# ScalarE's high halves of y for the first two groups, eight steps earlier, in a fused attention and feed-forward kernel

## The reference

```
q, k = l2norm(x Wq'), l2norm(x Wk')      # 16 heads of 16 values
attn = softmax(q k' - slope_h * distance), over the 128 keys up to and with the query
x = layernorm(x + (attn v) Wo')
h = gelu(x (alpha1 * sign(w1))' + b1)     # 1024 hidden values, alpha the mean |w| of a row
x = layernorm(x + h (alpha2 * sign(w2))' + b2)
```

## Time and profile before

| | |
|---|---|
| median of 3 runs | 369.43 us (369.34 to 369.77) |
| the profiled execution, its time | 370.22 us |
| its span, first to last instruction | 368.4 us |
| TensorE busy | 353.2 us, 96% of the span |
| VectorE busy | 308.7 us, 84% |
| ScalarE busy | 307.3 us, 83% |
| GpSimd busy | 285.4 us, 77% |
| granted TensorE clock, mean | 0.997 of full |

### The profile page before, as it was taken

How to read it: one execution, slowest core, us unless ns; L and a number is a source line. 1 busy time by engine, 2 the same in 40 slices (tenths; PEclk the granted TensorE clock), 3 DMA queues, 4 the chain that set the end, 5 groups by cost and what they waited for, 6 DMA issues and landing times. The chain is left out here.

```text
span 368.4 us, 13096 instructions
## 1 busy us (share of the span) xinstructions
PE 353.2 (96%) x4461; PEld 244.1 (66%) x4461; DVE 308.7 (84%) x771; ACT 307.3 (83%) x532; POOL 285.4 (77%) x440
## 2 busy tenths in 40 slices
PE   8789999999999999999999999999999999999992
PEld 5555676667766776776677677675666667667682
DVE  5977899898898898898899988879777887786775
ACT  3588888898898998898899999988888888887753
POOL 1188999889989999998999999757756856856433
PEclk9999999999999999999999999999999999999998
DMA  7678944744655646667767773303303513413113
GB/s 231 143 117 186 185 109 98 157 99 94 137 120 106 142 96 132 139 159 154 156 144 155 153 147 74 59 4 59 59 0 59 115 45 72 114 39 76 59 59 114
DMA packets 106884, 40.19 MB, mean 109 GB/s; under 512 B 92128, under 2 KB 105824, under 8 KB 106720
## 3 DMA queue, kind: packets, MB, share of 16 engines
q1 hardware_dynamic: 106848, 39.73, 49.6%
HBM read 12.72 MB, written 4.19 MB: 46 GB/s over the span
## 5 line engine op out<-in xcount | busy, mean ns | idle before, releaser
L1341 POOL TENSOR_SCALAR_AFFINE_SELECT prob<-prob 128x512 f32<-128x512 f32 x252 | 153.7, 646 | 11.1 <-ACT prob L700 11.1
L700 ACT ACTIVATE prob<-ps 128x1024 f32<-128x1024 f32 (+1 forms) x128 | 122.2, 1009 | 13.5 <-PE ps L390 13.4
L551 PE MATMUL ps<-yT,sgn 128*128 128x512 f16 x256 | 61.1, 379 | 0.0
L772 ACT ACTIVATE ps<-ps,bias,alpha 128x512 f32<-128x512 f32 x64 | 47.9, 750 | 15.6 <-PE ps L551 12.5
L421 PE MATMUL ps<-wqkv,xt 128*128 128x512 f32 x124 | 58.7, 596 | 1.2 <-DVE qkn L952 1.1
L411 PE MATMUL ps<-prob,vdiag 128*17 128x128 f32 x1024 | 51.3, 274 | 0.3
L411 PE MATMUL ps<-prob,vnext 128*17 128x128 f32 x992 | 49.9, 273 | 0.0
L1409 POOL TENSOR_TENSOR resid<-z,resid 128x256 f32 (+1 forms) x31 | 22.5, 726 | 29.9 <-DVE z L1173 29.9
L551 PEld LDWEIGHTS ps<-yT,sgn 128*128 128x128 f16 x256 | 25.0, 98 | 22.6
L390 PE MATMUL ps<-qkT 64*64 64x192 f16 (+2 forms) x1024 | 33.7, 248 | 2.8 <-DMA qkT<-parts 2.7
L454 PE MATMUL ps<-wo,oT 128*128 128x256 f32 x128 | 36.2, 405 | 0.1
(11 more groups left out here) (113 smaller groups left out, 690.2 us busy)
## 6 DMA issues: line engine op xcount, KB each, us to landing
xt<-in_xT SPq DMA_DIRECT2D x32, 128.0 KB, 2.1
resid<-in_x SPq DMA_DIRECT2D x32, 128.0 KB, 2.2
out_dram<-resid SPq DMA_DIRECT2D x7, 512.0 KB, 2.9
w<-in_w2T SPq DMA_DIRECT2D x1, 1024.0 KB, 7.7
w<-in_w1T SPq DMA_DIRECT2D x4, 256.0 KB, 3.3
w_nat<-in_w SPq DMA_DIRECT2D x4, 256.0 KB, 3.3
wqkv<-in_wqkvT SPq DMA_DIRECT2D x3, 256.0 KB, 3.9
qkT<-parts SPq DMA_TRANSPOSE x39, 4.3
```

Of the source, the lines that this page charges most:

```text
L551: mm = nc.tensor.matmul(ps[:, bank, :], sgn1[:, c, P * k:P * k + P], yT[:, par, a, c, :, :], start=(m == 0), stop=(m == 2 * DC - 1))
L700: nc.scalar.activation(to, scored, ACT.Exp, scale=QK_SCALE ** -2).then_inc(exp_done, 1)
L772: nc.scalar.activation(bank, bank, ACT.Gelu, bias=bias1[:, k:k + 1], scale=alpha1[:, k:k + 1]).then_inc(gelu_done, 1)
L1341: return nc.gpsimd.affine_select(out=at, in_=at, compare_op=ALU.is_ge, fill=0.0, base=-near, pattern=[[0, CH], [1 if near else -1, P]], ch ...
```

## The change

Only ScalarE's program changes. The function `high_y` moves up, unchanged. The loop makes three turns instead of five, so it covers steps 4 to 15. Steps 16 to 23 are written out, with `high_y` as their `tail`: blocks 0 to 3 in steps 16 to 19 and blocks 4 to 7 in steps 20 to 23. Steps 24 to 29 lose their `tail`, and `high_pair` goes from the drain. The signs (`amid`, `before_rows`) stay.

```diff
+            def high_y(n, b, par):
+
+                act.wait_ge(y_done, n * GB + b + 1)
+                count(act, y_in[par], (n - par) * 8)
+                nc.scalar.activation(yparts[:, par, 0, :, b, :], resid4[:, n * GB + b, :, :], ACT.Copy).then_inc(yhi_done, 1)
+
...
-            with act.Fori(0, (NB - 12) // XS) as t:
+            with act.Fori(0, (NB - 20) // XS) as t:
                 for n in range(XS):
                     step(t * XS + 4 + n, n)
...
+            for n in range(2):
+                for b in range(XS):
+                    step(NB - 16 + n * XS + b, b, tail=lambda n=n, b=b: high_y(n, b, n))
...
-            step(NB - 8, 0, amid=lambda: signs1(0), tail=lambda: high_y(0, 0, 0))
-            step(NB - 7, 1, amid=lambda: signs1(1), tail=lambda: high_y(0, 1, 0))
-            step(NB - 6, 2, amid=lambda: signs1(2), tail=lambda: high_y(0, 2, 0))
-            step(NB - 5, 3, amid=lambda: signs1(3), tail=lambda: high_y(0, 3, 0))
-            step(NB - 4, 0, amid=lambda: signs2(0), tail=lambda: high_y(1, 0, 1))
-            step(NB - 3, 1, next3=False, before_rows=lambda: signs2(1), tail=lambda: high_y(1, 1, 1))
+            step(NB - 8, 0, amid=lambda: signs1(0))
+            step(NB - 7, 1, amid=lambda: signs1(1))
+            step(NB - 6, 2, amid=lambda: signs1(2))
+            step(NB - 5, 3, amid=lambda: signs1(3))
+            step(NB - 4, 0, amid=lambda: signs2(0))
+            step(NB - 3, 1, next3=False, before_rows=lambda: signs2(1))
...
             take_strips(NB - 2)
-            high_pair()
             gelu_of(0, 3, 0)
```

More of the change, by code:

```diff
@@ L796, in activate @@
                         high_y(n + 1, 3, 1 - par)
-            def high_pair():
-                high_y(1, 2, 1)
-                high_y(1, 3, 1)
             def last_signs():
```

## The result

The changed kernel takes 371.52 us in the median of 12 runs, the kernel before 369.71 in the median of 12 runs beside it. The ratio is 1.0055, with a 95% interval of 1.0031 to 1.0080. The forecast was 371.0, between 369.2 and 372.4, and slower.

The account below looks back on a forecast made before the run. TensorE was taken to set the end throughout, so only its stalls between 129 and 257 us count. Terms 0.3 - 0.15 - 0.2 + 1.6 = +1.55 us on 369.43 gave 371.0, range 369.2 to 372.4.

Parts of the forecast that it names:

- The drain (+1.6): Drain: GpSimd's unbroken additions hold VectorE's small operations, so TensorE stands 1.6 us at block 30's rows (L445).
- The count of boundaries: Drain: each dependent small VectorE operation waits for the end of a GpSimd instruction, costing one GpSimd pitch; gives 1.6 us.
- L1126 did as put down: Drain, L1129 before the change: starts at 245.80, waits for the low half ending at 246.02, ends at 246.15 as before.
- The upper bound of 3.0: Drain: TensorE's stall reaches +3.0 us if L1129 and L961 each miss an end of a GpSimd instruction (0.65 and 0.69).
- Rival (b): Drain: GpSimd's additions don't hold the 128x1 operations, or VectorE slips between; the 1.6 falls away, 369.4 us; chance 0.18.
- Steps 16 to 23 (+0.3): ScalarE's eight copies there shift GpSimd's timing; cost between 0 and 0.58 us, middle +0.3 taken.
- in the same slack: Steps 16 to 23: dropping two of ScalarE's loop ends gains nothing, as they lie in ScalarE's wait for TensorE's scores.
- the wait for the third exponential: ScalarE, steps 17 to 24: its wait for TensorE's scores shrinks to 0.2 to 0.4 us instead of 0.5 to 0.7.
- Steps 24 to 30 (-0.35): Without ScalarE's copies in steps 24 to 29: -0.15 us in steps 24 to 27 and -0.2 in step 30.
- the forecast 0.2: Step 30: ScalarE reaches the signs up to 0.30 us earlier, so TensorE gains 0.2, between 0 and 0.30.
- The tight place: Drain: TensorE's turn of block 30's rows (L445) needs VectorE's normalised rows (L883), whose slack is 0.1 us.
- The sum: Whole kernel: 0.3 - 0.15 - 0.2 + 1.6 = +1.55 us, giving 371.0 from the median 369.43.

Follow-up runs that it names:

- six additions in the gap: Kernel before with six of GpSimd's eight bias additions moved into its 3.5 us idle time in the drain: 371.44 us against 369.81, ratio 1.0042.
- the pair early: Kernel before with only the high halves of blocks 6 and 7 moved from the drain to the ends of steps 30 and 31: 371.57 us against 369.81.
- the idle copies: Changed kernel with six same-size copies that nobody reads at the ends of steps 24 to 29: 371.97 us against 369.77 for the kernel before, ratio 1.0060.
- four additions in the gap: Kernel before with four of GpSimd's bias additions moved into its idle time in the drain: 370.41 us against 369.77, ratio 1.0013.

## Why the prediction was right, point by point

**The drain (+1.6).** Right in mechanism, place and size. L865, L867 and L869 each ended 0.02 us behind the end of one of GpSimd's additions (248.33, 249.02, 249.70), L958 0.16 behind the next (250.38). The stage took 1.51 longer and TensorE's wait was 1.45. The count of boundaries held operation by operation: from the first product's start to the row's end (L865 to L958) 2.75 us, against 1.06 before. L1126 did as put down: a low half ended in its course (246.27), and it kept its 0.35 us. The upper bound of 3.0 was not touched. Rival (b), that GpSimd's additions let the small operations pass, is refuted by four kernels: the changed one, the one with six additions in the gap, the one with the pair early and the one with the idle copies.

The Trainium skill's rule ("SBUF — State Buffer", section "Who interferes with whom") said for additions what my rows had only for cuts, and the runs agree: 0.56 to 0.66 us instead of 0.15. It also says that an operation with one SBUF input outside the two-port modes is not shut out. L1114 shows that: 0.15 us at 245.81, with a low half under way on GpSimd.

```profile
245.81 0.15 DVE L1114 TENSOR_SCALAR h_unscale<-h_scale 128x1 int32<-128x1 int32 x1
```

**Steps 16 to 23 (+0.3).** The sum was off by 0.4, since one term was missing. The copies cost 57.34 - 57.04 = 0.30, the middle that I had taken between two bounds. The size is steady (57.31 to 57.35 in four kernels with early copies), but by which path it reaches TensorE was not traced, so that the middle was hit is partly luck. The writing out, which I put at nothing "in the same slack", gave 57.45 - 57.04 = 0.41 back. I had named the path over GpSimd to VectorE for the copies and left it out for the loop.

One sign that I had named did not come: the wait for the third exponential was to shrink to 0.2 to 0.4 us. It stayed at 0.52 to 0.77 in steps 17 to 23, and only in step 24 was it 0.15. The slack that takes up the copy lies earlier. ScalarE in step 17, in the kernel with steps 16 to 23 written out and then in the changed one:

```profile
136.46 1.93 ACT L700 ACTIVATE prob<-ps 128x1024 f32<-128x1024 f32 x2
...
139.46 0.60 ACT L648 ACTIVATE sq<-ps 128x512 f32<-128x512 f32 x1 [0.23 <-PE ps L421]
...
140.84 1.94 ACT L700 ACTIVATE prob<-ps 128x1024 f32<-128x1024 f32 x2 [0.52 <-PE ps L390]
```
```profile
136.86 1.93 ACT L700 ACTIVATE prob<-ps 128x1024 f32<-128x1024 f32 x2
...
139.55 0.60 ACT L648 ACTIVATE sq<-ps 128x512 f32<-128x512 f32 x1
...
140.94 1.94 ACT L700 ACTIVATE prob<-ps 128x1024 f32<-128x1024 f32 x2 [0.52 <-PE ps L390]
```

TensorE's L454 of the step stands 0.10 us later in the second (136.23 and 136.13). Counted from it the first exponential is 0.30 late, and the squares (L648) are not late at all: ScalarE had waited for TensorE's projection there. So the third exponential does start when it did, as forecast, but the slack that makes it so is not the one that I named.

**Steps 24 to 30 (-0.35).** Not shown. The profile of the changed kernel says +0.39, but profiles of the same instructions differ by as much. In step 30 alone, the forecast 0.2 can be seen (6.36 us from the scores of step 30 to those of step 31, against 6.56), but the kernel with four additions in the gap, which has the old copies, took 6.36 too.

**The tight place.** That the slack of VectorE ahead of L883 was 0.1 us was the step that made the rest count: with 0.47 us more in one operation, four additions cost 0.33 of the time.

**The sum.** The profile says +1.80 where the sum said +1.55. The drain, 1.51 of it, was forecast for its reason. The rest came near by luck: steps 16 to 23 were 0.41 below their terms and steps 24 to 30 were 0.74 above theirs, and the two errors have opposite signs.

## What to carry to other kernels

An engine that idles off the critical path may be what keeps another engine fast. Before taking away a wait, ask what the freed engine will do in that time, and whose short operations run then: in a chain of tiny two-input operations on VectorE each one cost one GpSimd instruction here, however small it was. And if a change frees such work, a wait on the last of the short operations can hold it back; here that cost nothing.

A loop's end on an engine with slack need not be free if what follows it feeds another engine: writing out one loop of ScalarE gained 1.0 us here, while moving eight copies lost 1.8.

## What the runs showed of the hardware

VectorE's smallest operations with two inputs in SBUF last until GpSimd's instruction under way has ended: 0.15 us became 0.56 to 0.66 with additions of 0.69 to 0.71 in a row, and in the run with four additions the end of L868 followed the end of GpSimd's instruction by 0.02 us (247.03 and 247.01).

The end of a turn of ScalarE's loop costs 0.17 us without a releaser in its own timeline, and 0.2 us on the path. The Trainium skill has in "Runtime: NRT & Kernel Launch", section "Instruction fetch mechanics", that a taken branch breaks the sequential fetch of instructions and stalls when its target is not in the part at hand, and that this is one reason why kernels prefer to be written out where they can. That writing out can pay, ScalarE's loop shows (ratio 0.9973); for VectorE's and GpSimd's it made no difference, and with TensorE's the gain was no longer there (1.0001). Whether the 0.17 us are such a fetch no run here shows.
